# A group norm and masked batch norm kernel: six tiles' stores moved from ScalarE's queue to SyncE's, behind the last loads

## The reference

```python
def _gn(v, G=32, eps=1e-5):
    g = v.reshape(B_, G, C_ // G, H_, W_)
    m = jnp.mean(g, axis=(2, 3, 4), keepdims=True)
    s = jnp.var(g, axis=(2, 3, 4), keepdims=True)
    return ((g - m) / jnp.sqrt(s + eps)).reshape(v.shape)

# of _L0_conv_ref(x), with x = _gn(x)
m = x.sum(axis=1) != 0
...
inv = 1.0 / jnp.sqrt(var + EPS)          # by channel, over the places of m
out = jnp.where(m[:, None, :, :], x * inv[None, :, None, None], x)
...
x = x + _L0_conv_ref(_gn(x))
```

## Time and profile before

| | |
|---|---|
| median of 3 runs | 1277.55 us (1277.38 to 1278.63) |
| profiled execution, its time | 1278.15 us |
| profiled execution, its span | 1276.4 us |
| DMA queues | q1 (SP): 276.83 MB; q10 (ScalarE): 260.05 MB |
| mean rate | 421 GB/s |
| busy: TensorE, VectorE, ScalarE, GpSimd | 58%, 60%, 64%, 39% |

### The profile page before, as it was taken

How to read it: one execution, slowest core, us unless ns; L and a number is a source line. 1 busy time by engine, 2 the same in 40 slices (tenths; PEclk the granted TensorE clock), 3 DMA queues, 4 the chain that set the end, 5 groups by cost and what they waited for, 6 DMA issues and landing times.

```text
span 1276.4 us, 10694 instructions
## 1 busy us (share of the span) xinstructions
PE 743.7 (58%) x2882; PEld 303.7 (24%) x2882; DVE 764.6 (60%) x1894; ACT 816.3 (64%) x950; POOL 495.1 (39%) x504
## 2 busy tenths in 40 slices
PE   0777654576545675456765556654577545675436
PEld 0222221222212222222222222222122212222212
DVE  7766556565565566655665556556565665566634
ACT  0877555775556765567755578555776556775555
POOL 0055333453334443334433345333453334443330
PEclk9988767887768877678876788777887767877678
DMA  9999999999999999999999999999999999999976
GB/s 397 416 430 429 430 430 429 431 430 431 429 431 429 431 429 431 429 432 428 431 429 432 430 431 428 433 428 427 431 423 429 420 428 428 422 428 428 424 329 264
DMA packets 39084, 537.58 MB, mean 421 GB/s; under 512 B 4336, under 2 KB 4336, under 8 KB 6896
## 3 DMA queue, kind: packets, MB, share of 16 engines
q1 hardware_dynamic: 21168, 276.83, 51.2%
q10 hardware_dynamic: 17856, 260.05, 47.7%
HBM read 268.44 MB, written 268.44 MB: 421 GB/s over the span
## 4 chain that ended last, share of the span: by engine, by line
DMA 61%; ACT 17%; PE 10%; DVE 6%; issue 5%; SPq 0%; ACTq 0%; DVEq 0%
DMA out_dram<-slots 37%; DMA slots<-in_x_dram 24%; ACT slots L377 11%; PE flush L454 6%; ACT fresh L373 5%; DVE stats L508 2%; PE small_ps L417 1%; PE stay L450 1%; PE stay L451 1%; PE small_ps L427 1%; DVE spread L487 1%; PE small_ps L428 1%; ACT sums L373 0%; DVE dev L554 0%; DVE spread L528 0%
## 5 line engine op out<-in xcount | busy, mean ns | idle before, releaser
L508 DVE BATCH_NORM_STATS2 stats<-slots 128x6 f32<-128x512 f32 x1024 | 632.4, 681 | 458.0 <-DMA slots<-in_x_dram 456.5
L377 ACT ACTIVATE slots<-slots,out_bias,out_scale 128x1024 f32<-128x1024 f32 x512 | 623.1, 1247 | 2.0 <-DVE out_bias L565 1.2
L355 POOL TENSOR_TENSOR sums<-fresh,sums 128x512 f32<-128x512 f32 x360 | 459.2, 1275 | 374.9 <-ACT fresh L373 374.9
L454 PE MATMUL flush<-slots,weights 128*64 128x512 f32 x1536 | 443.6, 698 | 40.9 <-ACT fresh L373 39.3
L373 ACT ACTIVATE fresh<-flush,group_bias 128x512 f32<-128x512 f32 x360 | 247.7, 688 | 51.8 <-PE flush L454 51.8
L454 PEld LDWEIGHTS flush<-slots,weights 128*64 128x64 f32 x1536 | 132.1, 156 | 294.3 <-issue 293.5
L389 ACT ACTIVATE by_image<-by_image,eps 128x4 f32<-128x4 f32 x32 | 9.5, 297 | 262.6 <-DVE by_image L532 262.0
L333 POOL TENSOR_TENSOR weights<-pair_sum,group_rstd 128x64 f32<-128x64 f32 x128 | 33.7, 294 | 361.0 <-DVE group_bias L545 361.0
L417 PE MATMUL small_ps<-stats,group_avg 128*128 128x64 f32 x64 | 21.5, 436 | 207.1 <-DVEq L521 207.1
L450 PE MATMUL stay<-slots,weights 128*64 128x512 f32 x512 | 139.7, 605 | 0.0
L451 PE MATMUL stay<-minus_mean,weights 128*64 128x512 f32 x512 | 138.1, 593 | 0.0
(11 more groups left out here) (54 smaller groups left out, 203.5 us busy)
## 6 DMA issues: line engine op xcount, KB each, us to landing
slots<-in_x_dram SPq DMA_DIRECT2D x127, 2048.0 KB, 18.5
out_dram<-slots ACTq DMA_DIRECT2D x124, 2048.0 KB, 28.9
out_dram<-slots SPq DMA_DIRECT2D x16, 512.0 KB, 5.5
slots<-in_x_dram SPq DMA_DIRECT2D x4, 512.0 KB, 23.5
```

The costliest lines, as they stand in the source:

```text
L355: pool.tensor_tensor(into, fresh[:, n % FRESH_BUFS, :], into, ALU.add).then_inc(added, 1)
L377: nc.scalar.activation(out_in_ring(u, i), image_in_ring(u, i), ACT.Identity, bias=out_bias[:, u % 2, t:t + 1], scale=out_scale[:, u % 2, t ...
L454: nc.tensor.matmul(into, weight, source, start=True, stop=True).then_inc(image_summed, 1)
L508: last = V.bn_stats(stats[:, u % 2, k * BLOCK_STATS:(k + 1) * BLOCK_STATS], source)
```

## The change

Stores of tiles from `TILES - RING` (118) on are no longer issued by ScalarE. SP issues those of 118 to 123 behind the four chunks of tile 127 and ahead of the chunk stores of unit 31. Each still waits for its tile's outputs (`out_ready`) and counts on the same semaphore.

```diff
@@ sync engine, behind the loop over loads
+            for j in range(TILES - RING, TILES - UNIT_TILES):
+                sp.wait_ge(out_ready, (j + 1) * TILE_CHUNKS)
+                sp.dma_start(in_dram(out_rows, j), tile_in_ring(j)).then_inc(stored[j % RING], 16)
             for i in range(B):
                 sp.wait_ge(out_ready, LAST * B + i + 1)
                 sp.dma_start(chunk_in_dram(out_rows, LAST, i), out_in_ring(LAST, i)).then_inc(last_stored, 16)
@@ scalar engine
             def store(u, t):
                 j = u * UNIT_TILES + t
-                act.wait_ge(out_ready, (j + 1) * TILE_CHUNKS)
-                act.dma_start(in_dram(out_rows, j), tile_in_ring(j)).then_inc(stored[j % RING], 16)
+                if j < TILES - RING:
+                    act.wait_ge(out_ready, (j + 1) * TILE_CHUNKS)
+                    act.dma_start(in_dram(out_rows, j), tile_in_ring(j)).then_inc(stored[j % RING], 16)
```

## The result

The changed kernel takes 1269.56 us (median of 4 runs, 1269.2 to 1270.0), the kernel before 1277.8 (median of 4, the three shown above and one more beside the changed kernel). The ratio is 0.9934 with a 95% interval of 0.9921 to 0.9946. The forecast was 1269.7 in a range of 1267.5 to 1273.0.

What follows compares the result with a forecast made beforehand. DMA engines bound the kernel; only the stragglers' 7.9 us idle gap before the last chunk stores can be won. Closing it whole takes the median from 1277.55 to 1269.65 us (forecast 1269.7, range 1267.5 to 1273.0).

Steps and rivals of the forecast that it cites:

- the idle gap of the engines that finish last: Between tile 123's store and unit 31's chunk stores, stragglers idle from 1245.6 to 1253.5: 7.9 us, all a reordering can win.
- Alternation by rows: Engines take one row of each queue in turn, so a last-load chunk beside stores needs 8 x (0.613 + 0.165) = 6.2 us.
- The chain: Unit 31's statistics, from VectorE's last block through two products to ScalarE's root: 3.0 us, ready at 1228.1.
- The forecast for the first output: Unit 31's first output starts at 1236.0 instead of 1250.47, its chunk issued at 1237.3 with 7.1 us to spare.
- the root: ScalarE's root for unit 31 waits until ScalarE ends unit 30's outputs at 1230.7, the last of three gates.
- the wait on its slot: Unit 31's first output waits for tile 118's store, expected to land at 1221.7, ahead of 1236.
- the last stage: Unit 31's 16 chunk stores at the end take 22.0 us, from tile 123's end to the last landing.
- My own row count: Straggler's rows counted one by one: stores end at 1246.2 (measured 1245.6 used), chunk stage 16 x 8 x 0.165 = 21.1 us.
- Nothing is won: Rival, 3%: the last chunks' 6.1 us has another cause than store rows; last load stays at 1240.9, time 1277.5.
- The rival by which stores start one at a time: Rival, 3%: each SyncE store starts only when the one ahead has landed, 1.8 us extra per tile; time 1281.
- The partial case: Rival, 12%: the gap closes only in part, as with tile 118's store landing at 1246.5: 3.9 us won, 1273.7.
- the 14 early engines: They idle around 1200 to 1208 at no cost, finishing at 1266.0 against the stragglers' 1267.6, 1.6 us ahead.

Runs made afterwards that it cites:

- e3: Only the stores of tiles 121 to 123 moved to SyncE, against the kernel before: 1269.03 us, ratio 0.9934.
- e4: Kernel before with tile 127 loaded as one transfer of 16 KB rows, no store moved: 1268.73 us, ratio 0.9931.
- e5: Kernel before with all stores kept on ScalarE, those of tiles 118 and 119 issued later: 1269.19 us, ratio 0.993.
- e7: Changed kernel with unit 31 stored in four tiles of 16 KB rows instead of sixteen chunks: 1269.01 us, ratio 0.993 to the kernel before.
- e8: Kernel before with tile 127 loaded whole and unit 31 stored in four whole tiles, no store moving queue: 1269.2 us, ratio 0.9932.
- e9: The changed kernel run again, beside the kernel before: 1269.62 us, ratio 0.9937.
- e1: Only tile 123's store moved to SyncE, against the kernel before: 1277.46 us, ratio 1.0001.
- e6: Changed kernel with tile 118's store issued last of the six: 1273.78 us, ratio 0.9966 to the kernel before.

## Why the prediction was right

**The bound.** The forecast took the idle gap of the engines that finish last, 7.9 us, for all that can be won. The gain was 8.2 us (6.9 to 10.1 by the interval), and six kernels that close the gap (e3, e4, e5, e7, e8, and e9, the changed one again) lie within 1 us of each other, however they close it. That the figure is met within 0.3 us is partly luck, as the paragraph on the end shows.

**The last loads.** Alternation by rows was the step on which all rested, and it was an inference from one spacing. The prediction set the 85 GB/s of a chunk beside the pipe's 400; that is the pace of the engines that finish last alone. On nearly all others the chunks had gone by before 1222 us: from then to 1234 q1 moved only 0.17 MB. The dose test (0, 4.7, 8.4 us for one, two, three stores) and the whole load (9.7 us for 8 rows against 8) bear it out, both forecast in numbers. e5, with all stores on ScalarE, and e4, with no store moved, show that the move to SyncE's queue is not what counts.

**The chain.** The forecast for the first output was 1236.0, measured 1236.44; for the root 1230.7, measured 1231.14, held by ScalarE's own order as said. VectorE finished its blocks at 1221.1 (forecast 1221.3) and TensorE unit 30's sums at 1225.7 (1225.1). One term in between was off: the statistics' first steps took longer than before. Three rows of VectorE in the changed kernel, then three of GpSimd:

```profile
1226.41 0.56 DVE L529 TENSOR_SCALAR minus_mean<-group_mean 128x4 f32<-128x4 f32 x1
...
1227.41 1.33 DVE L532 SCALAR_TENSOR_TENSOR spread<-stats,spread 128x64 f32<-128x64 f32 x1
...
1229.57 0.82 DVE L540 TENSOR_SCALAR by_image<-by_image 128x4 f32<-128x4 f32 x1
...
1225.68 1.27 POOL L358 TENSOR_TENSOR sums<-fresh,sums 128x512 f32<-128x512 f32 x1 [1.55 <-ACT fresh L376]
1227.39 1.27 POOL L358 TENSOR_TENSOR sums<-fresh,sums 128x512 f32<-128x512 f32 x1 [0.44 <-ACT fresh L376]
1229.09 1.27 POOL L358 TENSOR_TENSOR sums<-fresh,sums 128x512 f32<-128x512 f32 x1 [0.44 <-ACT fresh L376]
```

VectorE's three took 0.17, 0.24 and 0.17 us before, when GpSimd was idle beside them. Here each starts during one of GpSimd's additions and ends within 0.1 us of that addition's end (1226.97 to 1226.95, 1228.74 to 1228.66, 1230.39 to 1230.36), as if held up by it. Not every step is held: the reduction at 1229.31 (L536), beside the same addition as the third, took its usual 0.22. The first two stand ahead of the root; the third does not. The chain was ready for the root at about 1229.5 instead of the 1228.1 forecast, and still ahead of 1231.1.

**The stores and the end.** Tile 118 landed at 1221.9 (forecast 1221.7), so the wait on its slot did not bite. Two terms of the sum were mis-sized, and by luck they nearly cancelled: tile 123 landed at 1247.0, where I took 1245.6, and the last stage then took 1267.3 - 1247.0 = 20.3 us, where I took 22.0. So the last landing moved by 7.9 - 1.4 + 1.7 = 8.2 us. My own row count had given 1246.2 and 21.1; I used the measured values of before in their place, and the counts would have been nearer in both. Of the 1.7 us, 0.9 is what the stage of before had above its row count. The rest fits a higher rate (21.1 x 401 / 415 = 20.4); the rows from 1254 to 1264 us, before and after:

```profile
1254.00:1264.00 10.00, 10.00 (x50) 4.47 (x48) 6.45 (x18) 10.00 (x9) 0.00 (x0) 1.00 1.02 401
...
1254.00:1264.00 10.00, 0.85 (x5) 0.30 (x2) 1.01 (x4) 0.66 (x1) 0.00 (x0) 0.79 1.02 415
```

Why the same 4 KB rows moved faster is open.

**The rivals.** "Nothing is won" would have needed a cause of the 6.1 us other than the stored rows; e1 to e4 exclude it. As for the section "Issuing engines are not separate DMA queues" of the Trainium skill's "DMA: Bandwidth & Descriptors": e5 (1269.19 with all stores on ScalarE) agrees that the issuing engine itself is worth nothing. The time of 1277.5 that the prediction tied to it did not come: e1 to e3 show that what stands beside the last loads was worth up to 8.4 us. The rival by which stores start one at a time fell with SyncE's six issues and their landings: tile 118 and tile 123 landed 25.1 us apart, 5.0 a tile, with no 1.8 us between them. The partial case, a late store of tile 118, is real as a mechanism (e6) and did not occur.

**The dip.** The prediction let the 14 early engines idle "for some us" at no cost as long as they stay 1.6 us ahead. It is 0.39 x 12 + 0.2 x 5 = 5.7 us of the whole pipe's time, larger than I had thought of. By the rows that follow, most of it is idle time that otherwise comes later, and so costs nothing. In e3 and e4, which have no dip, the share is down from 1237 to 1246 us, where it is 0.98 in the changed kernel:

```profile
1237.00:1246.00 9.00, 8.52 (x28) 3.39 (x30) 3.94 (x16) 6.22 (x7) 1.32 (x6) 0.61 0.47 190
...
1237.00:1246.00 9.00, 9.00 (x35) 3.43 (x36) 5.41 (x17) 7.46 (x8) 0.09 (x1) 0.78 0.59 235
```

That is 4.8 and 3.7 us of the pipe's time. The end shows how much lead the early engines have left: first e3, then e4, then two stretches of the changed kernel.

```profile
1262.00:1267.00 5.00, 0.00 (x0) 0.00 (x0) 0.00 (x0) 0.00 (x0) 0.00 (x0) 0.50 0.32 127
...
1262.00:1267.00 5.00, 0.00 (x0) 0.00 (x0) 0.00 (x0) 0.00 (x0) 0.00 (x0) 0.50 0.12 45
...
1262.00:1264.00 2.00, 0.00 (x0) 0.00 (x0) 0.00 (x0) 0.00 (x0) 0.00 (x0) 0.50 0.98 399
1264.00:1266.00 2.00, 0.00 (x0) 0.00 (x0) 0.00 (x0) 0.00 (x0) 0.00 (x0) 0.50 0.37 152
```

0.12 is again two engines of 16: in e4 the others are done by 1262, and two decide the end at 1267. In the changed kernel all are busy until 1264. With two at work to 1267, a share of 0.37 leaves the others an average end near 1264.6, some 2 us ahead of the last; the prediction had 1.6. So the lead has shrunk but isn't used up. I would expect that holding back much more from here on costs time; no run here tried it. That the two are always the same engines isn't shown, as the trace doesn't name them.

## What to carry to other kernels

When loads and stores share the DMA engines from two queues, they share them here by rows, not by bytes: on an engine that has both to do, a transfer in 4 KB rows beside one in 16 KB rows gets a fifth of the bytes (a chunk took 6.2 us instead of 1.3). Where the last transfer that a long chain waits for is cut finer than the traffic beside it, give it rows of the same size, or keep the other queue empty while it runs; here either was worth 8 us of 1278, and three moved stores did as much as six. What a reordering can win is about the idle time of the engines that finish last, so measure that gap first (7.9 us here, 8.2 won).

## What the runs showed of the hardware

The DMA engines are not equally far at the end of this kernel: two of 16 lag behind. In the kernel before, from 1238 to 1245 us only a share of 0.14 to 0.11 of the pipe was busy, with what was left of the last load and of tile 123's store, and since a transfer counts as landed only when the last engine reports, those two set the waits there. The early engines could stand idle for 5.7 us of the pipe's time without the kernel becoming measurably slower. Why two engines lag is open.

Short VectorE steps took up to five times as long (1.33 us against 0.24) beside GpSimd's additions, and each ended with the addition beside it; that GpSimd causes it was not tested apart.
